# Four places instead of two for an expert tile's rows, normalised in place and turned first in an iteration

## The reference, cut to what matters

```python
def _layernorm(x, axis=-1, eps=1e-05):
    m = jnp.mean(x, axis=axis, keepdims=True)
    v = jnp.var(x, axis=axis, keepdims=True)
    return (x - m) / jnp.sqrt(v + eps)
...
logits = x2 @ gate_w.T
probs = jax.nn.softmax(logits, axis=-1)
topk_vals, topk_idx = jax.lax.top_k(probs, TOP_K)          # TOP_K = 2 of 16
...
gu = jnp.einsum('th,eih->eti', x2, w_gate_up)              # 512 -> 2 * 128 per expert
g, u = jnp.split(gu, 2, axis=-1)
act = jax.nn.silu(g) * u
out_e = jnp.einsum('eti,ehi->eth', act, w_down)            # 128 -> 512
moe_out = jnp.einsum('eth,te->th', out_e, combine)
return (moe_out + shared_out).reshape(orig_shape)
...
x = x + jnp.tanh(g_ffn[2]) * _L2_ffn_ref(_layernorm(x, axis=-1), L2_ffn_gate_w, ...)
```

## Time and profile before

| | us |
|---|---|
| time of three runs | 2721.16, 2723.46, 2728.06 (median 2723.46) |
| profiled execution, its own time | 2720.39 |
| profiled execution, span in the trace | 2718.6 |
| first `turn2` begins, last `contract2` begins and takes | 1801.29, 1931.83 and 1.13 |

### The profile page before, as it was taken

How to read it: one execution, slowest core, us unless ns; L and a number is a source line. 1 busy time by engine, 2 the same in 40 slices (tenths; PEclk the granted TensorE clock), 3 DMA queues, 4 the chain that set the end, 5 groups by cost and what they waited for, 6 DMA issues and landing times.

```text
span 2718.6 us, 42172 instructions
## 1 busy us (share of the span) xinstructions
PE 2490.2 (92%) x13741; PEld 2091.4 (77%) x13741; DVE 1811.5 (67%) x3409; ACT 1263.7 (46%) x3698; POOL 1235.4 (45%) x1379
## 2 busy tenths in 40 slices
PE   4899999998889999999987888888689999999978
PEld 4788888887778888888765776765478888888854
DVE  3777777767777777777665776553477777776652
ACT  2445554554245555555434454223245555555421
POOL 4545445554234444444425666412444444444433
PEclk7999999999999999999999998899889999999979
DMA  4112222331112111111200000269501111110144
GB/s 121 46 49 93 90 94 83 102 102 55 48 62 91 36 40 36 32 36 33 66 20 16 1 1 26 97 199 321 166 27 48 37 32 40 40 36 21 44 176 161
DMA packets 67885, 191.68 MB, mean 71 GB/s; under 512 B 10097, under 2 KB 10737, under 8 KB 64730
## 3 DMA queue, kind: packets, MB, share of 16 engines
q1 hardware_dynamic: 51936, 139.85, 15.9%
q0 software_dynamic: 10224, 42.03, 4.5%
q10 hardware_dynamic: 5514, 7.11, 0.8%
HBM read 170.57 MB, written 52.14 MB: 82 GB/s over the span
## 4 chain that ended last, share of the span: by engine, by line
PE 77%; DVE 7%; POOL 6%; issue 5%; DMA 3%; ACT 2%; ACTq 0%; SPq 0%; POOLq 0%; DVEq 0%
PE B_qkv L748 30%; PE B_out L748 19%; PE B_oT L818 4%; PE B_s L798 4%; PE B_qT L788 3%; PE B_pt L808 3%; PE B_s L799 1%; PE B_out L1076 1%; PE B_qT L993 1%; DVE xn L1429 1%; PE B_oT L1076 1%; PE B_oT L892 1%; PE B_s L748 1%; PE B_qkv L993 1%; POOL ring_l L2048 1%
## 5 line engine op out<-in xcount | busy, mean ns | idle before, releaser
L1259 ACT ACTIVATE W<-S,nmx 128x128 f32<-128x128 f32 x768 | 297.6, 394 | 44.7 <-DVE nmx L1527 44.5
L2056 POOL TENSOR_SCALAR rn<-ss 128x5 f32<-128x5 f32 x128 | 25.6, 200 | 615.4 <-DVE ss L1470 615.4
L1156 ACT ACTIVATE sq<-B_qkv 128x640 f32<-128x640 f32 x128 | 90.1, 704 | 418.6 <-PE B_qkv L748 418.6
L2077 POOL TENSOR_TENSOR S<-S,mask 128x512 f32<-128x512 f32 x192 | 250.4, 1304 | 20.4 <-ACT S L1097 19.3
L1545 DVE SCALAR_TENSOR_TENSOR X<-B_out,gates,X 128x512 f32<-128x512 f32 x200 | 150.2, 751 | 164.0 <-PE B_out L748 163.9
L2116 POOL TENSOR_TENSOR W<-W,rden 128x512 f32<-128x512 f32 x192 | 199.9, 1041 | 83.4 <-DVE rden L1532 83.4
L748 PE MATMUL B_qkv<-ring_h,xnT_h 128*128 128x512 f32 x544 | 216.4, 398 | 8.3 <-DVE spare_l L1386 4.0
L748 PE MATMUL B_out<-ring_h,oT_h 128*128 128x512 f32 x516 | 207.9, 403 | 10.8 <-DVE kT L1517 6.5
L748 PE MATMUL B_qkv<-ring_l,xnT_h 128*128 128x512 f32 x544 | 215.1, 395 | 0.0
L748 PE MATMUL B_qkv<-ring_h,xnT_l 128*128 128x512 f32 x544 | 213.9, 393 | 0.0
L798 PE MATMUL B_s<-kT,qT_h 128*128 128x256 f32 x768 | 203.8, 342 | 10.6 <-DVE xnT_l L1386 9.9
(11 more groups left out here) (498 smaller groups left out, 7885.8 us busy)
## 6 DMA issues: line engine op xcount, KB each, us to landing
raw<-in_pieces SPq DMA_DIRECT2D x270, 256.0 KB, 2.7
slots_x<-in_zero SPq DMA_DIRECT2D x32, 1030.0 KB, 6.6
raw<-in_experts SPq DMA_DIRECT2D x16, 768.0 KB, 7.1
w<-in_experts SPq DMA_DIRECT2D x8, 1024.0 KB, 11.9
slots_y<-S SPq DMA_DIRECT2D x31, 256.0 KB, 6.0
sq<-slots_x ACTq DMA_DIRECT2D x8, 257.5 KB, 6.1
qk<-slots_x ACTq DMA_DIRECT2D x8, 257.5 KB, 6.8
raw<-in_ctxT SPq DMA_DIRECT2D x8, 256.0 KB, 2.7
```

Source lines behind the costliest of these rows:

```text
L1156: act.activation(sq[:, :], B_qkv[:, 0:HG + P], ACT.Square).then_inc(*squared.now((layer, u)))
L1259: t = act.activation(W[:, k, cols(r)], S[:, k, cols(r)], ACT.Exp, bias=nmx[:, k, r:r + 1], accum_out=den[:, k, r:r + 1])
L2077: pool.tensor_tensor(S3, S3, m.unsqueeze(1).to_broadcast([P, R, P]), ALU.add).then_inc(*masked.now((layer, u)))
```

## The change

Rows get four places: `sq`, `qk` and both halves of `xn`, which is made 3 numbers wider per half for it. `apply2` writes its result over its input instead of into `xn`, so its waits for a free half of `xn` are gone, and `turn2` reads the place. A place is free when its tile is turned, no longer when it is normalised, so the loads of rows wait for `turn2(t - 4)`. In the table the loads of rows stand two iterations earlier (tiles 2 and 3 are loaded with 0 and 1, ahead of the stage). `turn2` moves from place 30 to place 13 of its iteration, and `apply2` from place 12 of the same iteration to place 21 of the one before (tile 0 keeps its place).

```diff
-                self.at(*((first - 4, 0) if t < 2 else (first + t - 2, 31)), "load_rows2", t)
+                self.at(*((first - 4, 0) if t < 4 else (first + t - 4, 14)), "load_rows2", t)
             else:
-                self.at(first + t - 2, 9, "fetch_rows2", t)
+                self.at(first + t - 4, 9, "fetch_rows2", t)
...
-            self.at(first + t, 12, "apply2", t)
-            self.at(first + t, 30, "turn2", t)
+            self.at(*((first + t - 1, 21) if t else (first, 12)), "apply2", t)
+            self.at(first + t, 13, "turn2", t)
...
-        xn = sb("xn", [P, 2, D])
+        xn = sb("xn", [P, 2, XW])
...
-        rows2 = [m[:, 0:XW] for m in (sq, qk)]
+        rows2 = [sq[:, 0:XW], qk[:, 0:XW], xn[:, 0, :], xn[:, 1, :]]
...
-                    n = pe.transpose(B_pt[:, cols(c)], xn[:, t % 2, cols(c)], ident[:, :])
+                    n = pe.transpose(B_pt[:, cols(c)], rows2[t % 4][:, cols(c)], ident[:, :])
...
-                if t > 1:
-                    act.wait_ge(*row_normed.of((2, t - 2)))
+                if t > 3:
+                    act.wait_ge(*rows_turned.of((2, t - 4)))
+                elif t == 2:
+                    act.wait_ge(*ln_turned.of(("ffn2", NB - 1)))
...
-                row = rows2[t % 2]
+                row = rows2[t % 4]
                 dve.wait_ge(*rows2_in(t))
-                if t > 1:
-                    dve.wait_ge(*rows_turned.of((2, t - 2)))
-                elif t == 0:
-                    dve.wait_ge(*ln_turned.of(("ffn2", NB - 1)))
-                dve.tensor_scalar(xn[:, t % 2, :], row[:, 0:D], row[:, D:D + 1], row[:, D + 1:D + 2], ALU.subtract, ALU.mult
+                dve.tensor_scalar(row[:, 0:D], row[:, 0:D], row[:, D:D + 1], row[:, D + 1:D + 2], ALU.subtract, ALU.mult
...
-                pool.wait_ge(*row_normed.of((2, t - 2)))
-                pool.indirect_dma_start(out=rows2[t % 2], out_offset=None, in_=slots_x,
+                pool.wait_ge(*rows_turned.of((2, t - 4)))
+                pool.indirect_dma_start(out=rows2[t % 4], out_offset=None, in_=slots_x,
```

More of the change, by code:

```diff
@@ L676, in normed_rows @@
         def normed_rows(stage, b):
-            return xn[:, ln_place[stage, b], :]
+            return xn[:, ln_place[stage, b], 0:D]
         def mean_and_rstd(stage, b):
@@ L722, in rows2_in @@
         def rows2_in(t):
-            return x_in[4 + t % 2].of(("rows2", t)) if t < E2 else rows_in[t % 2].of((2, t))
+            return x_in[4 + t % 4].of(("rows2", t)) if t < E2 else rows_in[t % 4].of((2, t))
         def pick3(t):
@@ L1320, in load_rows2 @@
                         act.wait_ge(*rope_in[b].of(("slots", TOP2 - 1)))
-                act.dma_start(rows2[t % 2], slots_x[t * T:t * T + P, :]).then_inc(*x_in[4 + t % 2].now(("rows2", t)))
+                act.dma_start(rows2[t % 4], slots_x[t * T:t * T + P, :]).then_inc(*x_in[4 + t % 4].now(("rows2", t)))
             def expand2(t):
@@ L1997, in apply3 @@
                     dve.wait_ge(*ln_turned.of(("ffn3", NB - 1)))
-                dve.tensor_scalar(xn[:, t % 2, :], row[:, 0:D], row[:, D:D + 1], row[:, D + 1:D + 2], ALU.subtract, ALU.mult
+                dve.tensor_scalar(xn[:, t % 2, 0:D], row[:, 0:D], row[:, D:D + 1], row[:, D + 1:D + 2], ALU.subtract, ALU.mult
                                   ).then_inc(*row_normed.now(t))
@@ L2142, in fetch_rows2 @@
                     pool.wait_ge(*tabled.of("y_rows2"))
-                pool.wait_ge(*row_normed.of((2, t - 2)))
-                pool.indirect_dma_start(out=rows2[t % 2], out_offset=None, in_=slots_x,
+                pool.wait_ge(*rows_turned.of((2, t - 4)))
+                pool.indirect_dma_start(out=rows2[t % 4], out_offset=None, in_=slots_x,
                                         in_offset=bass.IndirectOffsetOnAxis(ap=row2_i[:, t - E2:t - E2 + 1], axis=0)
-                                        ).then_inc(*rows_in[t % 2].now((2, t)))
+                                        ).then_inc(*rows_in[t % 4].now((2, t)))
             def gather2(b):
```

## The result

| | before | after |
|---|---|---|
| time, median (runs) | 2724.03 us (2721.16 to 2728.06, 4 runs) | **2705.41 us** (2702.19 to 2708.00, 4 runs) |
| profiled execution, its own time | 2720.39 | 2702.19 |
| its span | 2718.6 | 2700.4 |
| `expand2(1)` to `expand2(30)`, us | 119.70 | 114.07 |

The ratio is 0.9936, 95% interval 0.9923 to 0.9950: 17 us faster (18.6 between the two medians) where 1.4 were forecast, and outside of the range of 2716 to 2728.5 us. Medians and ratios of this document leave out one execution of e8, which took 6247 us.

What follows compares the result with a forecast made beforehand. It took the third layer's expert tile cycle as the bound, with PE waiting 17.8 us for ACT's copy, plus late rows. Terms -3.55 + 1.5 + 1.5 - 0.9 = -1.4 us gave a median of 2722.0 us, range 2716 to 2728.5.

Steps and rivals of the forecast that it cites:

- The ring: Each expert tile: `expand2`, tanh, two products, `apply2`, `turn2`, `turn_act2`, next `expand2`; 4.06 us against 4.005, +1.5 us over 28 cycles.
- Late rows: Expert tiles whose rows land late: four places and earlier loads remove all such waits, -3.55 us.
- The start: Start of the expert stage: `turn2(1)` ahead of `expand2(0)` waits for the bank's copy, and `expand2(1)` begins later, +1.5 us.
- The end: End of the expert stage: no further tile to turn behind `expand2(29)`, 3.13 us instead of 4.02, -0.9 us.
- Rival 2: Expert stage: `apply2` is off PE's path and DMA sets the pace, 3.76 us a tile, -9.0 us to 2714.5; chance 0.06.
- Rival 1: Expert stage: DMA engines are the bound, late rows become late weights, the 3.55 us stay, 2725.6 us; chance 0.15.
- Rival 3: Expert stage: `apply2` waits until POOL's weight fetch is over, +0.90 us in 15 cycles, +13.5 to 2735.5; chance 0.07.

Runs made afterwards that it cites:

- e8: Kernel before with 32 bytes of padding ahead of `qk` and 32 more behind `r1`, order unchanged: 2710.70 us, ratio 0.9962.
- e1: Kernel before with `xn` as wide as in the changed kernel, order unchanged: 2715.46 us, ratio 0.9978.
- e5: Kernel before with 32 bytes of padding behind `r1`, moving only the big tensors: 2712.71 us, ratio 0.9958.
- e13: Kernel before with 160 bytes of padding behind `r1`: 2721.87 us in one run.
- e16: Kernel before with `mask13` and `ident` placed ahead of `qk` and 32 bytes of padding behind `r1`: 2709.84 us in one run.
- e2: Changed kernel with 32 bytes of padding behind `xn`, keeping the new order: 2718.33 us, ratio 0.9992 to the kernel before.
- e11: Changed kernel with 96 bytes of padding behind `xn`, keeping the new order: 2716.76 us, ratio 0.9979 to the kernel before.
- e12: Changed kernel with 64 bytes of padding behind `xn`, keeping the new order: 2715.19 us, ratio 0.9973 to the kernel before.
- e4: Changed kernel with `apply2` moved two places up, ahead of the two products of `expand2`: 2693.37 us, ratio 0.9903 to the kernel before.
- e18: e4 with 160 bytes of padding behind `r1`: 2705.10 us, ratio 0.9935 to the kernel before.
- e17: e4 with `mask2u` placed ahead of `qk` and 64 bytes of padding behind `r1`: 2685.95 us, ratio 0.9875 to the kernel before.
- e7: Kernel before with 32 bytes of padding ahead of `qk`, moving `oT` and ring together: 2720.53 us, ratio 0.9986.

## Why the prediction was wrong

- **The step that failed** is in its first paragraph: "Only there does the change move anything: apart from the moved rows, each engine's order is the same." The second half is true. The first does not follow from it, nor does the sentence ahead of the prediction that everything which the change moves lies in the stage or just ahead of it: the change moves tensors as well, all those behind `xn`. The sum has no term for the layout, so it put the output products of 192 attention units at nothing without a reason, and all rivals lie in the stage. That term is -11.5 us by the traces, and e1, e5 and e8, which have it alone, give 0.9967 as their weighted mean (interval 0.9959 to 0.9975), -9 us. e1 by itself is -6.0; its runs had a mean granted clock of 0.9639 where those of the kernel before beside them had 0.9666, and in the four samples of the kernel before 0.001 of clock goes with 1.2 to 1.3 us, which makes it -9.3.
- **The ring**: right in mechanism, mis-sized. I took 4.06 us where its own lower bound was 4.03; it is 3.965, below both. Three links are shorter than the rows that I took them from: second product to `apply2` 0.20 for 0.23, `turn2` to `turn_act2` 0.49 for 0.52, the last link 0.11 for 0.13. Why they are is not shown. 28 x (3.965 - 4.005) = -1.1 us in place of +1.5.
- **Late rows**: right that four places end them, no DVE wait for rows is left. Mis-sized, since the profiled execution was a lucky one: it lost 3.55 us to them, and the stages of nine other profiles with the old order (e1, e5 to e8, e13 to e16) lost 4.3 to 7.7, taken as there against 116.15. Late stores have a share in these losses that I did not separate.
- **The start**: +1.35 for +1.5. **The end**: 3.07 us instead of 4.02, -0.95 for -0.9. Both right.
- **Summed**: the order alone is -1.1 - 3.55 + 1.35 - 0.95 = -4.3 us in this pair of profiles. e2, e11 and e12 have it alone: 0.9982 as weighted mean (0.9976 to 0.9988), -5 us, with units of attention 0.004 us longer than before on the average (+0.8). So the order would have been near the forecast, and layout and order together -14 us by these runs and -16 by the traces. The two samples of the changed kernel give -18 (0.9933, 0.9922 to 0.9944). The 4 us between are at the edge of what the intervals leave; I can't say whether the whole is more than its parts. TensorE's clock in the profile after was at half speed for 169 us, and 193 before, which is where the 2.4 us may lie that the traces leave over. Over all runs that have it on record the mean granted clock is 0.9666 after and 0.9659 before, and 0.001 of it goes with 1.2 to 1.6 us, so that it explains 1 us of the 4.
- **Rival 2** took 3.76 us a tile as the DMA engines' floor, from a busy share of 0.94. e4 went under it, 3.54 us a tile, with a share of up to 1.00: the rate rose by more than the share. Its mechanism (`apply2` off PE's path) was no outcome of this change, but one edit away from it.
- **Rival 1** needs a full DMA; at 0.96 and 335 GB/s weights were in time in every tile after. **Rival 3**: beside a POOL fetch `apply2` took 0.54 us, as without; it was the fetch that grew, from 0.95 in the median of the 15 before to 1.10 us. In e4, where `apply2` stands elsewhere, it is 0.945 again. The exclusive lock that the Trainium skill describes (SBUF — State Buffer, "SBUF: two separate sides") may be seen in this, with DVE as its holder. It costs POOL 0.15 us, and PE nothing.

## What to carry to other kernels

An edit of a declaration is an edit of every tensor behind it. List the addresses before and after, and where a product of two operands runs thousands of times, look at its start-to-start time in both traces before explaining anything by the order of work. When such a product is slow with no wait in sight, shift one operand by 32 bytes a time: here 192 x 0.113 us, 0.8% of the time, lie by the units between the worst and the best distance (0.6% were measured between e18 and e17), for one line of padding. And when a ring is summed from links that were read in another order of work, their small errors add up: here 0.07 us too much in a cycle of 3.96.

## What the runs showed of the hardware

- Matmuls with fp32r operands, 128x128 held and 128x512 moved, start every 226 to 241 ns, according to the distance in memory of the two operands, not to the place of either (e5, e7, e8), and the products of the ring with `xnT`, whose distance no edit changed, kept their pace in all 20 traces. By the remainder of the distance by 256 the unit takes: 0: 9.447 to 9.460, 32: 9.547, 64: 9.487, 96: 9.560, 128: 9.553, 160: 9.540, 192: 9.533 or 9.540, 224: 9.547 us. That the repeat is by 256 was seen at two remainders only, 64 and 192. Why it is so stays open. The step that slows down ahead of the first `oT` product (226 ns after, 235 before) points at the load of the next held block beside the stream of the moved operand.
- The DMA engines moved 379 GB/s at a share of 1.00 in e4, and 352 at 1.01 in e17, where 0.94 had gone with 311 to 331: the share is no measure of what rate is left.
